# One of four masking chunks of a graph-attention stage moved from VectorE to GpSimd

## The chip, the cores and the metric

One core of a Trainium2 chip runs the whole program. The metric is the device time of one execution in microseconds (us). The engines are called as in the profile: PE (TensorE; PEld is its weight load), DVE (VectorE), ACT (ScalarE), POOL (GpSimd), SP (SyncE, here only an issuer of transfers; SPq is its queue).

## What is computed

A graph network of four layers on 3125 nodes and 100000 edges, of which only the first matters here. It is a stack of three graph-attention layers, and each does this:

```python
z = h @ W.T + b
e = leaky_relu(concat([z[src], z[dst]]) @ aW.T + ab, 0.01)[:, 0]
m = segment_max(e, dst)
ex = exp(e - m[dst])
alpha = ex / segment_sum(ex, dst)
return segment_sum(alpha[:, None] * z[src], dst)
```

## The kernel before

**Dense attention.** The kernel does not walk over edges here. It keeps a matrix of edge counts, sources by targets, in HBM, and computes a weight for every pair of a source and a target. A score depends on the source by one number and on the target by two, so that the exponent is a maximum of two sums: with s_low and s_rest of the source and two rows (shift_1, shift_2) of the targets, weight = exp(max(shift_1 + s_rest, shift_2) + s_low). It is clipped to at most 1 (a pair without an edge could otherwise be large) and multiplied by the count of edges, which is 0 for most pairs.

**Tiles and chunks.** `attention_layer` (line 899) is called once for each of the three layers. After a search for the maxima (line 1013, on DVE alone, 25 groups) comes the dense part: 25 source tiles of 128 rows (NT = 25), each cut into four chunks of target columns, `CUTS = (0, 512, 1536, 2560, 3125)`, so 512, 1024, 1024 and 565 columns. For tile s and chunk c there are four steps, each an instruction on its engine, and a fifth for the transfers:

- top (line 1030, DVE): `tops` = max(shift_1 + s_rest, shift_2), a scalar_tensor_tensor with two inputs in SBUF;
- exponentials (line 1074, ACT): exp in place in `tops`;
- mask (line 1039, DVE): `probs` = min(`tops`, 1) * `counts`, again a scalar_tensor_tensor with two inputs in SBUF;
- add_up (line 1106, PE): matmuls of z with `probs`, summed over the tiles in PSUM, two matmul records for each block of 512 columns;
- load_counts (line 949, SP): the counts of tile s + 1 into the same columns, once mask(s, c) is done.

`tops`, `probs` and `counts` are single buffers: top(s + 1, c) waits for mask(s, c), mask(s + 1, c) waits for add_up(s, c) (semaphore `used`) and for the load of the counts (semaphores `counts_in`), add_up(s, c) waits for mask(s, c). The semaphore `masked` counts all masks in order; DVE, PE and SP wait on it.

**Order on DVE.** A tile interleaves four tops with four masks two chunks back (`back`, line 941): top(s,0), mask(s-1,2), top(s,1), mask(s-1,3), top(s,2), mask(s,0), top(s,3), mask(s,1).

**POOL.** In the same stages POOL moves records of an edge table that a later part of the program needs. `StagedRows.scatter` (lines 477 to 485) waits for a load of 268 KB that SP issued (line 474) and issues four indirect DMAs of 128 rows (line 483). A layer's block on POOL is 6 of these jobs that go with the search and 14 that go with the dense tiles (`MOVED_DENSE`: in the layers 0 and 1 the even tiles and tile 11), with no other wait between them (lines 1091 and 1092); SP issues the loads for them before the counts of the tiles in `MOVED_DENSE` (line 974).

Of the kernel before, what the change touches and what calls it, by code (L numbers as in the profile page):

```python
# [10 lines left out]
ALU = mybir.AluOpType  # L11
# [10 lines left out]
NT = N // TN  # L22
# [28 lines left out]
MOVED_SEARCH = 6  # L51
MOVED_DENSE = ((11, *range(0, NT, 2)), (11, *range(0, NT, 2)), (0, 1, 2, 4, 6, 8, 9, 10, 12, 14, 16, 18, 20, 22))
# [8 lines left out]
NQ = len(CUTS) - 1  # L61
# [45 lines left out]
@contextmanager  # L107
def semaphores(nc, tag):

    held = []  # L110

    def sem(name):
        held.append(nc.alloc_semaphore(f"{tag}_{name}"))
        return held[-1]

    yield sem
    nc.clear_and_free_semaphores(held)
    nc.all_engine_barrier()  # L118
# [780 lines left out]
def attention_layer(k, layer, att):  # L899
# [10 lines left out]
    nc = k.nc  # L910
    tag, last_layer = f"a{layer}", layer == 2
    PER_BANK = 7
    with ExitStack() as ctx, semaphores(nc, tag) as sem:
        sb = lambda name, shape, dt=FP32: ctx.enter_context(nc.sbuf_tensor(f"{tag}_{name}", shape, dt))

# [3 lines left out]
        marks, marks_in, staged = att.marks_now, att.marks_in, att.staged  # L919
# [3 lines left out]
        counts, probs = sb("counts", [P, N]), sb("probs", [P, N])  # L923
        tops = sb("tops", [P, NPAD])
        chunk = [slice(a, b) for a, b in zip(CUTS, CUTS[1:])]
# [2 lines left out]
        shifts_in = [sem(f"shifts_in{c}") for c in range(NQ)]  # L928
        counts_in = [sem(f"counts_in{c}") for c in range(NQ)]
        topped, raised, masked, used = (sem(n) for n in ("topped", "raised", "masked", "used"))  # L930
        sums_taken, turned = sem("sums_taken"), sem("turned")
        sums = k.psum_cols(0, D + 1, N)
        sums_t = s_all[0:D + 1, 0:N]
# [3 lines left out]
        w_score, floor = sb("w_score", [D + 1, D]), sb("floor", [D + 1, 1])  # L937
        z_ready, sums_taken_act = sem("z_ready"), sem("sums_taken_act")
        TAKE = 3 * BANK

        def back(s, c):

            return (s, c - 2) if c >= 2 else (s - 1, c + NQ - 2)

        with nc.Block() as block:
            @block.sync
            def _(sp):
                def load_counts(s, c):
                    sp.dma_start(counts[:, chunk[c]], att.counts[s * P:(s + 1) * P, chunk[c]]).then_inc(counts_in[c], 16)

                sp.dma_start(s_all, att.score_rows[0, :].partition_broadcast(P)).then_inc(s_in, 16)
                with nc.allow_non_contiguous_dma(reason="a few thousand scores"):
                    sp.dma_start(d_group[:, :], att.score_rows[1, :].rearrange("(g p) -> p g", p=P)[0:GROUP, :])\
                        .then_inc(d_in, 16)
                for c in range(NQ):
                    load_counts(0, c)
                late = range(EARLY_MARKS, NGROUP // MARK_LOADS) if layer == 0 else ()
                for y in late:
                    att.load_marks(sp, y)
                    staged.load(sp)  # L960
                for _ in range(MOVED_SEARCH - len(late)):
                    staged.load(sp)

                sp.wait_ge(shift_step, 3)
                sp.dma_start(att.shift_rows.rearrange("a (g p) -> (a g) p", p=GROUP), shifts_t[:, 0:GROUP])\
                    .then_inc(rows_out, 16)
                sp.wait_ge(rows_out, 16)
                for c in range(NQ):
                    a, b = CUTS[c], CUTS[c + 1]
                    for to, row in ((shift_1, 0), (shift_2, 1)):  # L970
                        sp.dma_start(to[:, a:b], att.shift_rows[row, a:b].partition_broadcast(P))\
                            .then_inc(shifts_in[c], 16)
                for s in range(NT):
                    if s in MOVED_DENSE[layer]:
                        staged.load(sp)
                    for c in range(NQ):
                        if s + 1 < NT:

                            sp.wait_ge(masked, (s + 1) * NQ + c + 1)
                            load_counts(s + 1, c)  # L980

            @block.vector
            def _(dve):
                v, chain = nc.vector, Chain(dve, step)
                for sm in (raised, masked, used):
                    dve.sem_inc(sm, NQ)
                v.memset(shifts[:, :], 0.0)
                if not last_layer:
                    chain.link(v.memset(w_next[:, :], 0.0))
# [36 lines left out]

                def top(s, c):
                    cols = chunk[c]
                    dve.wait_ge(masked, s * NQ + c + 1)
                    v.scalar_tensor_tensor(tops[:, cols], shift_1[:, cols], s_rest[:, s:s + 1], shift_2[:, cols],  # L1030
                                           ALU.add, ALU.max).then_inc(topped, 1)

                def mask(s, c):
                    cols = chunk[c]
                    dve.wait_ge(raised, s * NQ + c + 1 + NQ)
                    dve.wait_ge(counts_in[c], s * 16 + 16)

                    dve.wait_ge(used, s * NQ + c + 1)
                    v.scalar_tensor_tensor(probs[:, cols], tops[:, cols], 1.0, counts[:, cols], ALU.min, ALU.mult)\  # L1039
                        .then_inc(masked, 1)  # L1040

                def tile(s, first=False):
                    for c in range(NQ):
                        if first:

                            dve.wait_ge(shifts_in[c], 32)
                        top(s, c)
                        if c >= 2 or not first:
                            mask(*back(s, c))

                for s in range(NT):
                    tile(s, s == 0)
                mask(NT - 1, NQ - 2)
                mask(NT - 1, NQ - 1)

                dve.wait_ge(used, NT * NQ + NQ)
                if last_layer:
                    v.tensor_copy(sums_t[:, 0:TAKE], sums[:, 0:TAKE]).then_inc(sums_taken, 1)
                else:
                    v.tensor_scalar(sums_t[:, 0:TAKE], sums[:, 0:TAKE], floor[:, :], 0.0, ALU.add, ALU.max)\  # L1060
                        .then_inc(sums_taken, 1)
                for b in range(0, NT, PER_BANK):
                    dve.wait_ge(turned, b // PER_BANK + 1)
                    n = min(PER_BANK, NT - b)
                    v.tensor_copy(k.acc[0:TN, b:b + n, 0:RESULT],
                                  k.psum[0:TN, b // PER_BANK, 0:n * RESULT].rearrange("p (t c) -> p t c", c=RESULT))

# [20 lines left out]

            @block.gpsimd
            def _(pool):  # L1090
                for _ in range(MOVED_SEARCH + len(MOVED_DENSE[layer])):
                    staged.scatter(pool)
                if last_layer:
                    staged.finish(pool)

            @block.tensor
            def _(pe):
                pe.wait_ge(shift_step, 1)
                nc.tensor.transpose(k.psum[0:2 * NGROUP, 7, 0:P], shifts[:, :], k.ident[:, :]).then_inc(shift_step, 1)  # L1099

                def add_up(s, c):

                    pe.wait_ge(masked, s * NQ + c + 1 + NQ)
                    for a in range(CUTS[c], CUTS[c + 1], BANK):
                        b = min(a + BANK, N)
                        last = nc.tensor.matmul(sums[:, a:b], k.z[:, s, 0:D + 1], probs[:, a:b], start=s == 0, stop=True,  # L1106
                                                skip_group_check=True)
                    last.then_inc(used, 1)

                if layer:  # L1110
                    pe.wait_ge(z_ready, 1)
                for s in range(NT):
                    for c in range(NQ):
                        add_up(s, c)

                pe.wait_ge(sums_taken, 1)
                if not last_layer:
                    pe.wait_ge(w_ready, 1)
                for t in range(NT):
                    at = (t % PER_BANK) * RESULT  # L1120
                    to, tile = k.psum[0:TN, t // PER_BANK, at:at + RESULT], sums_t[:, t * TN:(t + 1) * TN]
                    if t == TAKE // TN:
                        pe.wait_ge(sums_taken_act, 1)
                    if last_layer:
                        last = nc.tensor.transpose(to, tile, k.ident[0:D + 1, 0:D + 1])
                    else:
                        last = nc.tensor.matmul(to, tile, w_next[:, :], start=True, stop=True)
                    if t % PER_BANK == PER_BANK - 1 or t == NT - 1:
                        last.then_inc(turned, 1)
# [1064 lines left out]
```

## Time and profile before

| | us |
|---|---|
| device time, median of 3 runs (lowest, highest) | 4458.94 (4453.23, 4469.04) |
| the profiled execution: its span | 4502.7 |
| busy in the span: PE / DVE / ACT / POOL | 3132.8 / 3224.2 / 1435.4 / 1405.7 |
| a_probs (line 1039), 300 instructions, busy | 290.6 |
| a_tops on DVE (line 1030), 300 instructions, busy | 309.3 |
| records scattered on POOL (line 483), 192 + 96 instructions, busy | 327.6 + 166.6 |

The span is the one profiled execution from its first to its last instruction; it is the only time of that execution at hand, and lies 43.8 us (1.0%) above the median of the timed runs. A difference worked out from the profile is therefore added to the median as it is. Busy time of an engine that others wait for counts; idle time of another engine costs nothing. In the rows further down, "x" is a count, the number behind the bar is busy time and mean ns of one instruction, and "idle before" is how long the engine had been idle ahead of the instruction and for what it waited.

### The profile page before, as it was taken

What the parts mean: (1) busy time and instruction counts of PE and PEld (TensorE: products, weight loads), DVE (VectorE), ACT (ScalarE), POOL (GpSimd) and SP (SyncE); (2) the same over time, 40 slices, a digit from 0 to 9 for tenths busy, and PEclk for the clock granted to TensorE, in tenths of its full rate; (3) what the DMA queues carried; (4) which work ended last, traced back from release to release, by engine and by line L of the source; (5) the groups of instructions that cost most, each with busy time, mean ns of one, the idle gap of its engine ahead of it and who ended that gap; (6) DMA issues with size and microseconds to landing.
All of it is one profiled execution on the core that took longest, in us unless ns stands there. A gap on an engine that the chain in (4) does not pass through costs nothing. (4 is left out here: it accounts for less than half of the span.)

```text
span 4502.7 us, 84639 instructions
## 1 busy us (share of the span) xinstructions
PE 3132.8 (70%) x29061; PEld 2437.5 (54%) x29061; DVE 3224.2 (72%) x7791; ACT 1435.4 (32%) x2737; POOL 1405.7 (31%) x1198
## 2 busy tenths in 40 slices
PE   0087777777238348158499985588888769959995
PEld 0054444444102112112499984287888769959995
DVE  7766666665489699699577763377767579967886
ACT  0034444444025125035399981233333200000000
POOL 0055555555264454554000000266666300000000
PEclk9978888888569679579699996599999879979997
DMA  8845555545458358267377740111111024413331
GB/s 323 322 129 143 153 144 148 157 131 149 147 172 264 114 166 263 88 200 246 106 221 221 222 148 12 56 24 23 24 23 24 14 67 111 109 28 102 88 91 47
DMA packets 413507, 587.19 MB, mean 130 GB/s; under 512 B 76420, under 2 KB 301787, under 8 KB 412709
## 3 DMA queue, kind: packets, MB, share of 16 engines
q1 hardware_dynamic: 366005, 447.98, 34.2%
q0 software_dynamic: 37728, 66.91, 5.5%
q10 hardware_dynamic: 9360, 66.90, 3.7%
q8 instruction: 246, 4.03, 0.4%
q14 instruction: 168, 1.38, 0.1%
HBM read 340.05 MB, written 234.93 MB: 128 GB/s over the span
## 5 line engine op out<-in xcount | busy, mean ns | idle before, releaser
L846 POOL DMA_INDIRECT slots<-bc_rec,idx x496 | 484.6, 977 | 410.4 <-ACT bc_rec L807 294.4
L1284 POOL DMA_INDIRECT rp_rows<-rel_rows,slot_rel x390 | 412.1, 1057 | 431.7 <-POOLq L118 182.3
L1106 PE MATMUL psum<-a_probs,z 128*65 128x512 f32 (+1 forms) x1050 | 445.7, 557 | 145.0 <-DVE a_probs L1039 145.0
L1320 DVE TENSOR_SCALAR rp_hot_src<-rp_key_rows,lane 128x384 bf16<-128x384 f16 x1560 | 383.5, 317 | 202.0 <-issue 88.5
L1534 PE MATMUL psum<-rel_pieces,rp_hot_src 128*128 128x192 bf16 x4680 | 452.1, 249 | 94.3 <-issue 75.8
L1074 ACT ACTIVATE a_tops<-a_tops,a_s_low 128x1024 f32<-128x1024 f32 (+2 forms) x300 | 284.1, 947 | 569.6 <-DVE a_tops L1030 569.1
L1534 PEld LDWEIGHTS psum<-rel_pieces,rp_hot_src 128*128 128x128 bf16 x4680 | 390.4, 99 | 128.8 <-issue 107.0
L483 POOL DMA_INDIRECT slots<-h,idx x192 | 327.6, 1706 | 352.3 <-DMA h<-recs 304.1
L1106 PEld LDWEIGHTS psum<-a_probs,z 128*65 128x65 f32 x1050 | 121.8, 137 | 469.4 <-DVE a_probs L1039 301.5
L703 DVE TENSOR_SCALAR bc_first_t<-bc_ramp,bc_key_t 128x128 f16<-128x128 f16 x500 | 136.5, 273 | 307.8 <-PE psum L729 172.7
L1030 DVE SCALAR_TENSOR_TENSOR a_tops<-table,a_s_rest,big 128x1024 f32<-128x1024 f32 (+2 forms) x300 | 309.3, 1031 | 32.8 <-DMA big<-shift_rows 32.8
L729 PE MATMUL psum<-bc_first_s,bc_first_t 128*128 128x512 f16 x1000 | 220.2, 382 | 104.5 <-DVE bc_first_s L704 62.8
L1039 DVE SCALAR_TENSOR_TENSOR a_probs<-a_tops,a_counts 128x1024 f32<-128x1024 f32 (+2 forms) x300 | 290.6, 970 | 0.0
L1568 PE MATMUL psum<-ep_msg,ep_hot_dst 128*84 128x131 f32 x1950 | 278.4, 278 | 7.7 <-ACT ep_msg L1463 5.7
L1568 PE MATMUL psum<-sp_msg,sp_hot_dst 128*84 128x128 f32 x1950 | 280.6, 281 | 0.0
L1568 PE MATMUL psum<-sq_msg,sq_hot_dst 128*84 128x128 f32 x1950 | 272.0, 276 | 0.0
L704 DVE TENSOR_SCALAR bc_first_s<-bc_ramp,bc_key_s,bc_base_s 128x625 f16<-128x625 f16 x500 | 241.0, 482 | 0.8 <-issue 0.6
L1541 PE MATMUL psum<-far_pieces,sq_hot_src 128*128 128x128 bf16 x2925 | 217.7, 220 | 28.8 <-DMA sq_hot_src<-hot_rows 28.8
L1099 PE MATMUL psum<-ident,a_shifts 128*50 128x128 f32 x3 | 1.2, 411 | 331.3 <-DVE a_shifts L1021 331.3
L1541 PE MATMUL psum<-edge_pieces,ep_hot_src 128*128 128x131 bf16 x2925 | 229.1, 223 | 1.3 <-ACT ep_hot_src L1480 1.2
L792 ACT ACTIVATE bc_counts<-psum 128x625 f32<-128x625 f32 x125 | 88.2, 706 | 439.0 <-PE psum L739 232.2
L1568 PEld LDWEIGHTS psum<-ep_msg,ep_hot_dst 128*84 128x84 f32 x1950 | 221.7, 154 | 10.2 <-DVE ep_hot_dst L1329 9.9
(438 smaller groups left out, 6855.1 us busy)
## 6 DMA issues: line engine op xcount, KB each, us to landing
a_counts<-edge_counts SPq DMA_DIRECT2D x150, 512.0 KB
slots<-big ACTq DMA_DIRECT2D x65, 1005.0 KB
ep_rec<-slots SPq DMA_DIRECT2D x65, 1005.0 KB, 6.2
edge_counts<-bc_counts SPq DMA_DIRECT2D x12, 3125.0 KB
hot_rows<-ep_hot_src SPq DMA_DIRECT2D x325, 96.0 KB, 4.5
sp_hot_src<-hot_rows SPq DMA_DIRECT2D x325, 96.0 KB, 2.0
sq_hot_src<-hot_rows SPq DMA_DIRECT2D x325, 96.0 KB, 2.0
a_counts<-edge_counts SPq DMA_DIRECT2D x75, 282.5 KB
```

What stands on the lines that cost most here:

```text
L483: pool.indirect_dma_start(k.slots, bass.IndirectOffsetOnAxis(k.idx[:, at:at + 1], 0), self.rows[y][:, t, :], None).then_inc(self.scattered ...
L704: last = v.tensor_scalar(to_s[:, u, :], ramp[:, :], column(key_s, t), column(base_s, j), ALU.subtract, ALU.is_equal)
L846: pool.indirect_dma_start(k.slots, bass.IndirectOffsetOnAxis(k.idx[:, first + t:first + t + 1], 0), rec[:, j, t, :], None).then_inc(scatte ...
L1030: v.scalar_tensor_tensor(tops[:, cols], shift_1[:, cols], s_rest[:, s:s + 1], shift_2[:, cols], ALU.add, ALU.max).then_inc(topped, 1)
L1039: v.scalar_tensor_tensor(probs[:, cols], tops[:, cols], 1.0, counts[:, cols], ALU.min, ALU.mult)\
L1074: nc.scalar.activation(tops[:, cols], tops[:, cols], ACT.Exp, bias=s_low[:, s:s + 1])\
L1106: last = nc.tensor.matmul(sums[:, a:b], k.z[:, s, 0:D + 1], probs[:, a:b], start=s == 0, stop=True, skip_group_check=True)
L1284: pool.indirect_dma_start(rows[:, n % ROW_SLOTS, s, 0:width], None, table, bass.IndirectOffsetOnAxis(k.slot_rel[:, at:at + 1], 0))\
L1320: last = v.tensor_scalar(hot_src[:, n % HOT_SLOTS, rel, :], key_rows[:, n % 2, :], k.lane[:, rel:rel + 1], None, ALU.is_equal)
L1534: last = nc.tensor.matmul(to, hot_src[:, n % HOT_SLOTS, r, s * P:(s + 1) * P], pieces[:, row, r, :], start=s != 1 and r == 0, stop=True, s ...
L1541: last = nc.tensor.matmul(got[:, s, :], hot_src[:, n % HOT_SLOTS, s * P:(s + 1) * P], pieces[:, row, piece, :], start=s == 0 and piece == ...
L1568: last = nc.tensor.matmul(to[:, 0:D] if relations else to, hot_dst[:, y, s, :], got, start=first, stop=True, skip_group_check=True)
```

## The change

The third chunk (c = 2, columns 1536 to 2559) of every tile is masked on POOL, in two instructions (a tensor_scalar that clips in place in `tops`, and a tensor_tensor that multiplies by the counts into `probs`), with a semaphore between them. DVE keeps the masks of the chunks 0, 1 and 3. The waits are split: `masked` now counts DVE's three masks of a tile, `masked_pool` POOL's one; `wait_masked` picks between them for SP, DVE and PE. POOL's scatters of the dense part stand each behind the mask of its tile.

```diff
+    POOL_CHUNK = 2
+    MASKED_BY_DVE = [c for c in range(NQ) if c != POOL_CHUNK]
...
+        def wait_masked(eng, s, c):
+            if c == POOL_CHUNK:
+                eng.wait_ge(masked_pool, s + 2)
+            else:
+                eng.wait_ge(masked, (s + 1) * (NQ - 1) + MASKED_BY_DVE.index(c) + 1)
...
@@ SP, load_counts
-                            sp.wait_ge(masked, (s + 1) * NQ + c + 1)
+                            wait_masked(sp, s, c)
...
@@ DVE
-                for sm in (raised, masked, used):
+                for sm in (raised, used):
                     dve.sem_inc(sm, NQ)
+                dve.sem_inc(masked, NQ - 1)
+                dve.sem_inc(masked_pool, 1)
...
                 def top(s, c):
-                    dve.wait_ge(masked, s * NQ + c + 1)
+                    wait_masked(dve, s - 1, c)
...
-                        if c >= 2 or not first:
+                        if (c >= 2 or not first) and back(s, c)[1] != POOL_CHUNK:
                             mask(*back(s, c))
...
-                mask(NT - 1, NQ - 2)
                 mask(NT - 1, NQ - 1)
...
@@ POOL
-                for _ in range(MOVED_SEARCH + len(MOVED_DENSE[layer])):
+                def mask(s):
+                    cols = chunk[POOL_CHUNK]
+                    pool.wait_ge(raised, s * NQ + POOL_CHUNK + 1 + NQ)
+                    pool.wait_ge(counts_in[POOL_CHUNK], s * 16 + 16)
+                    pool.wait_ge(used, s * NQ + POOL_CHUNK + 1)
+                    nc.gpsimd.tensor_scalar(tops[:, cols], tops[:, cols], 1.0, None, ALU.min).then_inc(clipped, 1)
+                    pool.wait_ge(clipped, s + 1)
+                    nc.gpsimd.tensor_tensor(probs[:, cols], tops[:, cols], counts[:, cols], ALU.mult)\
+                        .then_inc(masked_pool, 1)
+
+                for _ in range(MOVED_SEARCH):
                     staged.scatter(pool)
+                for s in range(NT):
+                    mask(s)
+                    if s in MOVED_DENSE[layer]:
+                        staged.scatter(pool)
...
@@ PE, add_up
-                    pe.wait_ge(masked, s * NQ + c + 1 + NQ)
+                    wait_masked(pe, s, c)
```

## Rows read from the trace of the kernel before

**Rows 1.** Busy time by stretch: a search with the nodes before it, then a dense stage.

```profile
core 0: us, PE busy (x) PEld busy (x) DVE busy (x) ACT busy (x) POOL busy (x), PEclk, DMA share, GB/s
1160.00:1299.00 139.00, 7.72 (x31) 5.91 (x31) 99.37 (x85) 1.98 (x2) 68.10 (x34) 0.50 0.38 123
1299.00:1487.00 188.00, 145.81 (x343) 39.74 (x344) 182.15 (x200) 94.71 (x100) 79.14 (x55) 0.97 0.84 258
```

**Rows 2.** What DVE waited for, 1299 to 2135 us: total us, times, longest.

```profile
DVE a_tops L1030 <- DMA big<-shift_rows: 32.8, 9, 6.4
```

**Rows 3.** Instructions in order of time, 1324 to 1333 us (start, us, engine line).

```profile
1324.31 0.75 DVE L1030 SCALAR_TENSOR_TENSOR a_tops<-table,a_s_rest,big 128x512 f32<-128x512 f32 x1
...
1324.98 1.22 DVE L1039 SCALAR_TENSOR_TENSOR a_probs<-a_tops,a_counts 128x1024 f32<-128x1024 f32 x1
...
1325.51 1.52 POOL L483 DMA_INDIRECT slots<-h,idx  x1 [10.03 <-DMA h<-recs]
1326.11 1.28 DVE L1030 SCALAR_TENSOR_TENSOR a_tops<-table,a_s_rest,big 128x1024 f32<-128x1024 f32 x1
...
1327.31 0.75 DVE L1039 SCALAR_TENSOR_TENSOR a_probs<-a_tops,a_counts 128x565 f32<-128x565 f32 x1
1327.34 1.55 POOL L483 DMA_INDIRECT slots<-h,idx  x1 [0.30 <-issue]
...
1327.96 1.29 DVE L1030 SCALAR_TENSOR_TENSOR a_tops<-table,a_s_rest,big 128x1024 f32<-128x1024 f32 x1
...
1329.16 0.69 DVE L1039 SCALAR_TENSOR_TENSOR a_probs<-a_tops,a_counts 128x512 f32<-128x512 f32 x1
1329.19 1.49 POOL L483 DMA_INDIRECT slots<-h,idx  x1 [0.30 <-issue]
...
1329.76 0.81 DVE L1030 SCALAR_TENSOR_TENSOR a_tops<-table,a_s_rest,big 128x565 f32<-128x565 f32 x1
...
1330.48 1.23 DVE L1039 SCALAR_TENSOR_TENSOR a_probs<-a_tops,a_counts 128x1024 f32<-128x1024 f32 x1
...
1331.61 0.76 DVE L1030 SCALAR_TENSOR_TENSOR a_tops<-table,a_s_rest,big 128x512 f32<-128x512 f32 x1
```

**Rows 4.** Groups by shape, 1280 to 2180 us, all three dense stages.

```profile
L483 POOL DMA_INDIRECT slots<-h,idx x168 | 285.3, 1698 | 264.4 <-DMA h<-recs 222.1 <-issue 42.4
L1030 DVE SCALAR_TENSOR_TENSOR a_tops<-table,a_s_rest,big 128x1024 f32<-128x1024 f32 x150 | 192.5, 1283 | 14.5 <-DMA big<-shift_rows 14.5
L1039 DVE SCALAR_TENSOR_TENSOR a_probs<-a_tops,a_counts 128x1024 f32<-128x1024 f32 x150 | 183.2, 1223 | 0.0
L1074 ACT ACTIVATE a_tops<-a_tops,a_s_low 128x1024 f32<-128x1024 f32 x150 | 172.4, 1149 | 183.1 <-DVE a_tops L1030 183.1
...
L1013 DVE CUSTOM_DVE_ANT_0 a_tops<-marks_now,table 125x3200 f32<-125x3200 uint8 x28 | 97.6, 3485 | 6.9 <-issue 6.9
```

**Rows 5.** POOL in order of time: one scatter within the search, one behind it.

```profile
1284.68 3.11 POOL L483 DMA_INDIRECT slots<-h,idx  x1 [0.30 <-issue]
...
1292.77 0.96 POOL L483 DMA_INDIRECT slots<-h,idx  x1 [0.30 <-issue]
```

**Rows 6.** POOL's own computing instructions, whole program, by shape.

```profile
L266 POOL IOTA all_rows<- 128x3200 int16 x1 | 2.9, 2887 | 0.0
...
L269 POOL TENSOR_SCALAR_AFFINE_SELECT ident<-ident 128x128 f32<-128x128 f32 x1 | 0.3, 284 | 0.0
...
L261 POOL MEMSET ident<- 128x128 f32 x1 | 0.2, 204 | 0.3 <-POOLq L2187 0.3
...
L2187 POOL MEMSET const-float32-0.0<- 128x1 f32 x1 | 0.1, 98 | 0.3 <-issue 0.3
```

**Rows 7.** SP in order of time: loads of records in two tiles with jobs.

```profile
1321.15 0.43 SPq L474 DMA_DIRECT2D h<-recs  x1
1335.75 0.43 SPq L474 DMA_DIRECT2D node_midT<-recs  x1
```

**Rows 8.** PE's weight loads in order of time, from the third dense stage's start.

```profile
1958.61 0.23 PEld L1106 LDWEIGHTS psum<-a_probs,z 128*65 128x65 f32 x1 [0.62 <-issue]
1959.46 0.14 PEld L1106 LDWEIGHTS psum<-a_probs,z 128*65 128x65 f32 x1 [0.62 <-issue]
1959.89 0.14 PEld L1106 LDWEIGHTS psum<-a_probs,z 128*65 128x65 f32 x1 [0.29 <-issue]
```

More of the change, by code:

```diff
@@ L930, in attention_layer @@
         topped, raised, masked, used = (sem(n) for n in ("topped", "raised", "masked", "used"))
+        masked_pool, clipped = sem("masked_pool"), sem("clipped")
         sums_taken, turned = sem("sums_taken"), sem("turned")
```

## The prediction, made before the changed kernel was run

> **What bounds the kernel now.** I began with the busy time by stretch, since the change touches one kind of stage only. In the dense stage DVE is busy 182.15 of 188 us, PE 145.81, ACT 94.71 and POOL 79.14 [rows 1]; there are three such stages of nearly the same length, one eighth of the span. Next the list of what DVE waited for: in these stretches its longest entry is the load of the shift rows at each start, 32.8 us in 9 waits [rows 2], and no entry is a wait for ACT, PE or a count inside the tiles. So DVE sets the pace. Then the instructions in order of time: from top(s,0) at 1324.31 to the next one at 1331.61 the eight DVE instructions take 7.30 us [rows 3], less than the sum of their durations, since the record of one begins about 0.08 before that of the last one ends. The loads of records two tiles apart, at 1321.15 and 1335.75, give the same: 14.60 for two [rows 7]. What a mask of 1024 columns occupies is thus not its 1.22 us but the step from its start to the next start: 1324.98 to 1326.11, 1.13 us [rows 3].
>
> **What goes.** One such mask in each of 75 tiles: DVE's tile falls from 7.30 to 6.17 us, 85 us in all, if nothing else holds it.
>
> **What comes: POOL's two instructions.** The trace has no clip and no product on POOL, so I bound them by what POOL does compute [rows 6]. A memset of one column takes 98 ns, of 128 columns 204; an iota of 3200 columns 2887, so (2887 - 98) / 3200 = 0.87 ns a column; an affine_select, which reads and writes each element, (284 - 98) / 128 = 1.45 ns a column. The clip of 1024 columns lies between 0.10 + 0.89 = 0.99 us and 0.10 + 1.49 = 1.59; it is a read and a write without affine_select's test, so nearer the lower end, and I take 1.1. The product reads two elements for each it writes: at the least 0.99, with two passes at iota's rate 0.10 + 2 x 0.89 = 1.88, with two at affine_select's 0.10 + 2 x 1.49 = 3.07; I take 2.3, a little under the middle of the last two, as there is no test. Together 3.4 us a tile (2.9 to 4.7), for 1.13 us taken from DVE. The Trainium skill, GPSIMD Engine Reference, section "Elementwise — side-by-side cycle accounting", gives 4497 ns for a float32 tensor_tensor of 2048 columns, which would make about 2.25 us here, an estimate; by it the sum would come out 0.05 us a tile lower.
>
> **What POOL and DVE do to each other.** This I read from the scatters. A scatter takes 0.96 us when DVE is idle, and 3.11 plus 0.30 of issue when DVE runs the search's instructions of 3.49 us [rows 5, 4]: one scatter for each DVE instruction. In the dense stage the three in [rows 3] end at 1327.03, 1328.89 and 1330.68, each 0.92 or 0.93 us after a top began, 1326.11, 1327.96 and 1329.76, whatever the scatter's own start was. So a scatter that begins under a DVE instruction with two SBUF inputs waits until that has ended and then needs its usual time. It reads only an index a partition, and DVE's steps are not longer for it, so the trace doesn't show the other direction: whether a long POOL read holds DVE. The bounds are 0 and POOL's whole 3.4 us a tile. The Trainium skill, SBUF — State Buffer, section "SBUF: two separate sides", says it does: one shared pair of ports, held for a whole instruction by a VectorE instruction with two SBUF inputs or by a GpSimd instruction that reads SBUF, whichever came first. No row here shows that half of it.
>
> **The sum, first way (they exclude each other).** All seven DVE instructions left in a tile have two SBUF inputs. Tile = 6.17 + 1.1 + 2.3 + 0.2 for two changes of hands (DVE loses its overlap of about 0.1 each time) = 9.8 us, against 7.30.
>
> **The sum, second way (only POOL waits).** `tops` is one buffer, so chunk 2 is a ring: top(s,2) 1.28, exp 1.15 [rows 4], clip 1.1, product 2.3, and top(s+1,2) again. Before, DVE's order hid it. With some 0.1 for each of four semaphores it is 6.2 us, and POOL waits twice for the DVE instruction under way, about 0.5 each (half of 0.65 to 1.2): 7.2 us. That is for a tile without a job. With one, four scatters stand between this product and the next clip, in POOL's one queue: at the pace of [rows 3], (1.55 + 0.30) or (1.49 + 0.30) each, they take 7.3 us, longer than the 2.6 us until tops is ready again, and the ring is 7.3 + 0.5 + 1.1 + 0.1 + 0.5 + 2.3 = 11.8 us. Queued behind the late clip are the product, and behind that DVE's top(s+1,2) with all its later tops, PE's add_up of chunks 2 and 3, and SP's load of the next counts. A stage: 14 x 11.8 + 11 x 7.2 = 244 us, 9.8 a tile. Both ways meet at the same figure, so it does not hang on the unseen half of the exclusion.
>
> **What lies beside it.** SP now waits for POOL before counts(s+1,2) and, behind it in the same queue, counts(s+1,3) and the next load of records. A load of records took from 1321.15 to 1325.51, 4.4 us [rows 7, 3]; the counts of a chunk are twice as large. The clip waits for them as well, so they may replace the 2.6 us of top and exp in the ring of a tile without a job by 4.5 or so. I add 0.1 us a tile of the possible 0.8 (11 tiles of 25, 1.9 us). PE needs 12 records of 0.43 us in a tile [rows 8], about 5.5 us, and hides in 9.8. ACT (3.8 us a tile) hides too. The six search jobs are issued before the first mask, as before, and the last job of a stage ends beside the turning of the sums, so the edges cost nothing beyond a microsecond or two. The split semaphores are as many waits as before; the new `clipped` wait is in the 0.1s above. Nothing outside these stages changes.
>
> Sum: (9.9 - 7.3) x 75 = +195 us. Against the profiled execution that is 4502.7 + 195 = 4698; against the median of the runs 4458.9 + 195 = 4654, and the forecast is in terms of the median. A measurement of this kernel can tell about 0.3%, 13 us, from no change.
>
> **The rivals.**
> (A) The forecast, chance 0.70. With POOL's pair at 2.9 us it gives 4459 + 195 - 0.5 x 75 = 4616; at 4.7 it gives 4654 + 1.3 x 75 = 4751.
> (B) POOL's computing instructions run freely beside DVE, and only the ring and the queue behind the scatters cost. For it: the scatters show only an index read being held. Against: a product reads far more than an index. The ring is 6.2 without a job and 7.3 + 1.1 + 0.1 + 2.3 = 10.8 with one: 14 x 10.8 + 11 x 6.2 = 219 us against 182.5, +37 a stage, +110: 4569. Chance 0.17.
> (C) PE's clock falls. Now it is granted 0.97 in the dense stage and 0.50 in the search before it [rows 1]. If the gaps that POOL's late product leaves bring it to the lower level (1.2 GHz), weight loads are 0.85 us apart (1958.61 to 1959.46) in place of 0.43 [rows 8]; 12 of them and the two short ones make 10.6 us, more than the tile: +3.3 x 75 = +248, 4707. Against: PE would still be busy for more than half of the time. Chance 0.07.
> (D) Faster: POOL is hidden and DVE's 6.17 is the pace, -1.13 x 75 = -85, 4374. It decides on POOL's work in a stage: 25 pairs and 14 jobs must fit in 25 x 6.17 = 154 us to have all of it, and in 182 to have any. With 3.4 us and jobs at the unhindered pace (4 x 1.26 = 5.0) that would be 85 + 71 = 156; at the pace of [rows 3] it is 85 + 102 = 187, already over. It needs free running of both kinds, and the ring of the tiles with jobs (5.0 + 3.4 = 8.5) made up by those without. The scatters in [rows 3] speak against it. Chance 0.06.
>
> **The numbers.** The forecast is A's, 4654. The range takes in B at the low end with a little room, C, and A's upper bound: 4555 to 4755; outside are D and some of A's and B's tails. Faster by over 0.3%: 0.05, nearly all of D. Within 0.3%: 0.03, D in part and the easiest end of B. Slower: 0.92.
>
> **What would show it.** Right: dense stages of about 245 us; DVE no longer busy throughout, or with single tops and masks whose records are stretched to 3 us or more where they met POOL's product (exclusion, both directions); starts of top(s,0) about 10 us apart, farther in tiles with a job; a new wait of DVE's top of chunk 2 for POOL; the other stages unchanged. A top or mask that runs its 1.3 us in the middle of POOL's product would refute the exclusion and leave B. The whole would be wrong if POOL's pair took 2 us or less, or if the scatters fell to 0.96 us beside DVE; and the cost would be higher if PE's granted clock in the dense stage fell below 0.9.

## The result, and the profile after

The changed kernel takes 4778.4 us (median of 4 runs, 4775.7 to 4782.2) against 4458.9 of the kernel before: ratio 1.073, 95% interval 1.071 to 1.074, +319.5 us. The sign was forecast, the size not: +195 was expected and 4755 was the upper end of the range.

Busy time by stretch of the changed kernel: its three dense stages, with a search and the nodes between the first two.

```profile
core 0: us, PE busy (x) PEld busy (x) DVE busy (x) ACT busy (x) POOL busy (x), PEclk, DMA share, GB/s
1281.00:1577.00 296.00, 180.56 (x350) 52.57 (x350) 167.36 (x176) 94.73 (x101) 227.43 (x109) 0.78 0.52 165
1577.00:1708.00 131.00, 9.77 (x56) 8.45 (x56) 96.42 (x86) 2.81 (x2) 83.53 (x38) 0.52 0.24 71
1708.00:2006.00 298.00, 177.71 (x350) 51.36 (x350) 166.05 (x176) 95.05 (x101) 227.09 (x106) 0.78 0.51 163
2140.00:2437.00 297.00, 179.12 (x350) 51.72 (x350) 166.62 (x176) 94.89 (x101) 227.17 (x106) 0.78 0.51 163
```

Against [rows 1] the stage went from 188 to 296 us and DVE from busy all the time to 167 of 296. POOL, at 227, is the busiest engine, and is still idle for a quarter. PE's granted clock fell from 0.97 to 0.78. The stretch between is no longer than before. From here on a stage is measured in one way for every kernel: from its first top to the DVE instruction that takes the sums out of PSUM, mean of the three. It is 190.5 us before and 296.7 after; 3 x 106.2 = 319 us, the whole difference.

Groups by shape, 1280 to 2500 us, and below them what waited for whom in the same stretch (total us, times, longest).

```profile
L483 POOL DMA_INDIRECT slots<-h,idx x161 | 295.1, 1833 | 79.8 <-issue 41.1 <-DMA h<-recs 35.4 <-PE psum L1131 2.4
L1107 POOL TENSOR_SCALAR a_tops<-a_tops 128x1024 f32<-128x1024 f32 x75 | 219.8, 2931 | 166.0 <-DMA a_counts<-edge_counts 94.8 <-PE psum L1131 35.3 <-ACT a_tops L1085 34.7
L1042 DVE SCALAR_TENSOR_TENSOR a_tops<-table,a_s_rest,big 128x1024 f32<-128x1024 f32 x150 | 211.5, 1410 | 364.7 <-POOL a_probs L1109 351.2 <-DMA big<-shift_rows 13.6
L1109 POOL TENSOR_TENSOR a_probs<-a_tops,a_counts 128x1024 f32<-128x1024 f32 x75 | 177.9, 2372 | 6.3
```

```profile
DVE a_tops L1042 <- POOL a_probs L1109: 351.2, 71, 7.4
PE psum L1131 <- POOL a_probs L1109: 325.9, 75, 7.9
POOL a_tops L1107 <- DMA a_counts<-edge_counts: 94.8, 23, 5.5
POOL a_tops L1107 <- PE psum L1131: 35.3, 9, 3.9
```

DVE's top of chunk 2 now waits for POOL's product in 71 of 75 tiles, 4.9 us each: the new wait that was named. The product takes 2.37 us, as costed (2.3). The clip takes 2.93 us where 1.1 was put, and that is no effect of waiting: where DVE was idle it takes 2.79.

How a tile goes shows in the order of time. First one without a job; from product to product it takes 9.48 us (1398.41 to 1407.89).

```profile
1398.41 2.34 POOL L1109 TENSOR_TENSOR a_probs<-a_tops,a_counts 128x1024 f32<-128x1024 f32 x1
...
1400.78 1.28 DVE L1042 SCALAR_TENSOR_TENSOR a_tops<-table,a_s_rest,big 128x1024 f32<-128x1024 f32 x1 [6.36 <-POOL a_probs L1109]
...
1402.10 1.15 ACT L1085 ACTIVATE a_tops<-a_tops,a_s_low 128x1024 f32<-128x1024 f32 x1 [7.52 <-DVE a_tops L1042]
...
1404.44 2.72 DVE L1042 SCALAR_TENSOR_TENSOR a_tops<-table,a_s_rest,big 128x512 f32<-128x512 f32 x2
1404.67 3.14 POOL L1107 TENSOR_SCALAR a_tops<-a_tops 128x1024 f32<-128x1024 f32 x1 [3.92 <-PE psum L1131]
...
1407.89 2.34 POOL L1109 TENSOR_TENSOR a_probs<-a_tops,a_counts 128x1024 f32<-128x1024 f32 x1
```

The ring of the forecast is there, but its first part is another one: exp is done at 1403.25, yet the clip starts at 1404.67, when PE's add_up of this chunk ends. So it is in 9 tiles; in 23 others the clip starts when the counts land. PE began those four matmuls at 1400.80 after an idle of 7.27 us, and its weight loads there stand 0.85 us apart, the spacing of the lower clock level (1.2 GHz) in [rows 8]:

```profile
1401.71 0.23 PEld L1131 LDWEIGHTS psum<-a_probs,z 128*65 128x65 f32 x1 [0.62 <-issue]
1402.57 0.23 PEld L1131 LDWEIGHTS psum<-a_probs,z 128*65 128x65 f32 x1 [0.62 <-issue]
1403.42 0.23 PEld L1131 LDWEIGHTS psum<-a_probs,z 128*65 128x65 f32 x1 [0.62 <-issue]
```

The next tile has a job. First the view of POOL alone, then that of DVE alone:

```profile
1407.89 2.34 POOL L1109 TENSOR_TENSOR a_probs<-a_tops,a_counts 128x1024 f32<-128x1024 f32 x1
1410.39 2.10 POOL L483 DMA_INDIRECT slots<-node_midT,idx  x1 [0.16 <-issue]
1412.80 2.04 POOL L483 DMA_INDIRECT slots<-node_midT,idx  x1 [0.30 <-issue]
1415.14 2.22 POOL L483 DMA_INDIRECT slots<-node_midT,idx  x1 [0.30 <-PE psum L1131]
1417.66 0.98 POOL L483 DMA_INDIRECT slots<-node_midT,idx  x1 [0.30 <-issue]
1418.67 2.79 POOL L1107 TENSOR_SCALAR a_tops<-a_tops 128x1024 f32<-128x1024 f32 x1
1421.55 2.34 POOL L1109 TENSOR_TENSOR a_probs<-a_tops,a_counts 128x1024 f32<-128x1024 f32 x1
```

```profile
1415.78 0.74 DVE L1051 SCALAR_TENSOR_TENSOR a_probs<-a_tops,a_counts 128x565 f32<-128x565 f32 x1
1423.92 1.28 DVE L1042 SCALAR_TENSOR_TENSOR a_tops<-table,a_s_rest,big 128x1024 f32<-128x1024 f32 x1 [7.39 <-POOL a_probs L1109]
```

From product to product this tile takes 13.66 us, with four scatters in 8.3 between product and clip. DVE has nothing to do from 1416.5 to 1423.9 and the clip still needs 2.79.

### The profile page after: what moved, and what is told of

It is laid out like the page before. It is cut to its first block and busy times, and to the rows that moved or that the text cites. A ratio compares the mean times of both kernels' runs of the same rounds, so it can differ in the third digit from the quotient of the medians.

```text
span 4774.0 us, 84717 instructions
## 1 busy us (share of the span) xinstructions
PE 3207.6 (67%) x29061; PEld 2460.1 (52%) x29061; DVE 3173.5 (66%) x7716; ACT 1440.5 (30%) x2737; POOL 1822.7 (38%) x1348
## 5 line engine op out<-in xcount | busy, mean ns | idle before, releaser
L1131 PE MATMUL psum<-a_probs,z 128*65 128x512 f32 (+1 forms) x1050 | 537.4, 672 | 372.8 <-POOL a_probs L1109 325.9
L1042 DVE SCALAR_TENSOR_TENSOR a_tops<-table,a_s_rest,big 128x1024 f32<-128x1024 f32 (+2 forms) x300 | 324.0, 1099 | 383.9 <-POOL a_probs L1109 351.2
L1309 POOL DMA_INDIRECT rp_rows<-rel_rows,slot_rel x390 | 398.4, 1022 | 417.4 <-POOLq L118 181.2
L1131 PEld LDWEIGHTS psum<-a_probs,z 128*65 128x65 f32 x1050 | 155.6, 169 | 755.1 <-POOL a_probs L1109 393.6
L1559 PE MATMUL psum<-rel_pieces,rp_hot_src 128*128 128x192 bf16 x4680 | 437.8, 248 | 74.7 <-issue 46.9
L483 POOL DMA_INDIRECT slots<-h,idx x192 | 347.0, 1807 | 172.3 <-DMA h<-recs 120.0
L1107 POOL TENSOR_SCALAR a_tops<-a_tops 128x1024 f32<-128x1024 f32 x75 | 219.8, 2931 | 166.0 <-DMA a_counts<-edge_counts 94.8
L704 DVE TENSOR_SCALAR bc_more_s<-bc_ramp,bc_key_s,bc_base_s 128x625 f16<-128x625 f16 x500 | 224.0, 448 | 0.4 <-issue 0.4
```

The source lines that it names most:

```text
L483: pool.indirect_dma_start(k.slots, bass.IndirectOffsetOnAxis(k.idx[:, at:at + 1], 0), self.rows[y][:, t, :], None).then_inc(self.scattered ...
L704: last = v.tensor_scalar(to_s[:, u, :], ramp[:, :], column(key_s, t), column(base_s, j), ALU.subtract, ALU.is_equal)
L1309: pool.indirect_dma_start(rows[:, n % ROW_SLOTS, s, 0:width], None, table, bass.IndirectOffsetOnAxis(k.slot_rel[:, at:at + 1], 0))\
L1559: last = nc.tensor.matmul(to, hot_src[:, n % HOT_SLOTS, r, s * P:(s + 1) * P], pieces[:, row, r, :], start=s != 1 and r == 0, stop=True, s ...
```

## The experiments

Two theories explained about equally well a tile of 11.4 us (the mean distance from one first top to the next). *Ring*: POOL's chain of chunk 2 (its product, then what frees the clip, clip, product), with the scatters in its queue, sets the pace. *Exclusion*: POOL and DVE take turns, so all their work adds up, 6.17 + 2.79 + 2.34 + 0.2 = 11.5. The stage lengths in one place (us; before 190.5, after 296.7):

```
without the clip            219.7      control: jobs first, before 190.4
clip twice                  369.7      jobs first, changed kernel  250.0
waits behind the clip       281.7      control + free clips        217.4
chunk 0 on POOL             240.9      control + free products     268.3
clip as multiplication      280.8      control + free memsets      190.5
```

The kernel before took 4484 us where it ran beside the first three kernels, 4458 beside the next four and 4162 beside the last three. A dense stage in which DVE is undisturbed did not take part in that: it is 190.4 us long in the second group (jobs first, kernel before) and 190.5 in the third (free memsets). So times are compared only with the kernel before of the same group.

**The clip left out and doubled.**

```diff
-                    nc.gpsimd.tensor_scalar(tops[:, cols], tops[:, cols], 1.0, None, ALU.min).then_inc(clipped, 1)
-                    pool.wait_ge(clipped, s + 1)
```

> The changed kernel without POOL's clip: the product alone (the weights are then not cut at 1, a part of the computation that is left out). Ring theory: POOL's chain of chunk 2 sets the pace, so a tile without a job falls from 9.5 us to about 3.9 + 2.34 = 6.3, one with a job from 13.2 to about 10.4, a stage from 297 us to about 218, the time from 4778 to about 4545. Exclusion theory (POOL and DVE take turns, all their work adds up): a tile is 6.17 + 2.34 + 0.1 = 8.6 with or without a job, a stage about 220: the same total, but another pattern of the tiles.

Measured 4572.9 us, +89 over the kernel before (ratio 1.020, 1.017 to 1.023), so 230 less than the change costs. The total came out (stage 219.7 for 218), the pattern did not follow the ring alone: most tiles take 8.3 or 8.6 us, with or without a job. DVE's view shows why.

```profile
1438.88 4.04 DVE L1042 SCALAR_TENSOR_TENSOR a_tops<-table,a_s_rest,big 128x512 f32<-128x512 f32 x2
...
1449.01 2.89 DVE L1051 SCALAR_TENSOR_TENSOR a_probs<-a_tops,a_counts 128x565 f32<-128x565 f32 x1
```

```profile
1438.91 2.92 POOL L1107 TENSOR_TENSOR a_probs<-a_tops,a_counts 128x1024 f32<-128x1024 f32 x1 [3.73 <-DMA a_counts<-edge_counts]
...
1448.74 2.55 POOL L1107 TENSOR_TENSOR a_probs<-a_tops,a_counts 128x1024 f32<-128x1024 f32 x1
```

With the ring shorter, DVE works while POOL multiplies, and pays. The two tops at 1438.88 take 4.04 us where they take 1.94 without a product beside them; the mask of 565 columns takes 2.89 where 0.74 is usual. The product is longer by no more than the rest of the DVE instruction under way. So in this kernel the tile is the one that exclusion gives (8.6), and not the ring's 6.3 and 10.4: with the clip gone, exclusion by the product is what keeps the kernel slower than before.

```diff
-                    pool.wait_ge(clipped, s + 1)
+                    pool.wait_ge(clipped, 2 * s + 1)
+                    nc.gpsimd.tensor_scalar(tops[:, cols], tops[:, cols], 1.0, None, ALU.min).then_inc(clipped, 1)
+                    pool.wait_ge(clipped, 2 * s + 2)
```

> The changed kernel with the clip done twice. Ring theory: + (2.79 to 3.14 + 0.09) us in each of 75 tiles, +215 to +240 us, about 5005; DVE's additional instructions do not grow in number and it idles longer. Should the clip's cost be hidden in part, less.

Measured 4988.7, +505 over the kernel before (1.113, 1.110 to 1.116), 185 more than the change costs; by the stages it is 3 x 73.0 = 219, and the profiled execution had the longest span of its runs (5026). The second clips take 2.78 us each, 2.9 a tile with the wait: nothing of them is hidden.

**The waits moved behind the clip.**

```diff
-                    pool.wait_ge(counts_in[POOL_CHUNK], s * 16 + 16)
-                    pool.wait_ge(used, s * NQ + POOL_CHUNK + 1)
                     nc.gpsimd.tensor_scalar(tops[:, cols], tops[:, cols], 1.0, None, ALU.min).then_inc(clipped, 1)
                     pool.wait_ge(clipped, s + 1)
+                    pool.wait_ge(counts_in[POOL_CHUNK], s * 16 + 16)
+                    pool.wait_ge(used, s * NQ + POOL_CHUNK + 1)
```

> The changed kernel with POOL's waits for the counts and for PE's add_up put between clip and product. Ring theory: in the 33 tiles without a job the clip starts 2.5 us after the product before it (top and exp) instead of 3.9, so 9.5 becomes about 8.0; tiles with a job do not change, as the scatters end later than either. 33 x 1.4 = -46 us, about 4732. Exclusion theory: no change, since all the work still adds up.

Measured 4763.1, +279 over the kernel before (1.062, 1.059 to 1.065): 40 less than the change costs, 45 by the stages. The sum came out by luck, for its parts did not. Tiles without a job fell only from 9.5 to 9.3, those with one from about 13.2 to 12.4.

```profile
1410.77 2.34 POOL L1109 TENSOR_TENSOR a_probs<-a_tops,a_counts 128x1024 f32<-128x1024 f32 x1
1415.70 3.81 POOL L1105 TENSOR_SCALAR a_tops<-a_tops 128x1024 f32<-128x1024 f32 x1 [2.59 <-ACT a_tops L1085]
1419.59 2.79 POOL L1109 TENSOR_TENSOR a_probs<-a_tops,a_counts 128x1024 f32<-128x1024 f32 x1
```

The clip starts 2.6 us after the product, as expected; but now it meets more of DVE's instructions and takes 3.81, and the product 2.79. Why scatters in tiles with a job got shorter here was not tried; they begin at another point of DVE's sequence.

**The jobs moved in front.** In the kernel before and in the changed one, the 14 jobs of a stage go ahead of its first mask (`MOVED_SEARCH = 20`, `MOVED_DENSE = ((), (), ())`).

> Control: the kernel before with the 14 jobs of a dense stage moved in front of its first mask (POOL's queue and SP's loads). What counts is the length of the dense stage in the trace, not the time, which grows by the moved jobs. Both theories: 190 us as before, DVE's 7.30 a tile.

> The changed kernel with the same move of the jobs: no scatter stands between two masks of POOL. Ring theory: every tile takes the 9.5 us that tiles without a job take now, a stage about 245 us instead of 297. Exclusion theory: the scatters cost DVE nothing, a tile is 6.17 + 2.79 + 2.34 + 0.2 = 11.5, a stage about 290.

The control's stages are 190.4 us with 7.3 a tile, as with the jobs in them (190.5): the scatters never cost DVE anything. The changed kernel's are 250.0, nearly all tiles 9.5 us. Exclusion had 290. This is the run that tells the two apart: the pace was the ring's, and the 14 jobs are worth 47 us a stage in it. (The times, 4651 and 4823, hold the moved jobs too.)

**POOL's instructions by themselves.** The control with 60 instructions a stage on tensors that nobody else uses. Shown is the kernel with clips. In the other two the line with `tensor_scalar` is `nc.gpsimd.tensor_tensor(idle_out, idle_a, idle_b, ALU.mult)` or `nc.gpsimd.memset(idle_out, 0.0)`, with the same semaphore behind it.

```diff
+        idle_a, idle_b = (k.x[:, t:t + 10, :].rearrange("p t c -> p (t c)") for t in (0, 10))
+        idle_out, idle_step = k.node_in[:, :, :].rearrange("p t c -> p (t c)"), sem("idle_step")
...
+                pool.wait_ge(raised, 1 + NQ)
+                for i in range(60):
+                    if i:
+                        pool.wait_ge(idle_step, i)
+                    nc.gpsimd.tensor_scalar(idle_out, idle_a, 1.0, None, ALU.min).then_inc(idle_step, 1)
```

> The control with 60 clips of 640 columns a stage on POOL, on tensors that nobody else uses, one behind the other, waiting for nothing but the clip before. Each should take about 0.1 + 640 x 2.63 ns = 1.8 us. Exclusion: the stage grows from 190 by 60 x 1.8 = 108 us to about 298. No contention: 190. What the changed kernel's trace shows (a DVE instruction of 1.28 us takes 1.9 under a clip): in between, some 20 to 30 us.

> The same with 60 products of 640 columns with two inputs, about 1.5 us each. Exclusion: the stage grows by 60 x 1.5 = 90 us to about 280. No contention: 190.

> As the free clips and products, with 60 memsets of 640 columns a stage, which only write. If DVE loses time only where both read through something shared, its tile stays 7.30 us; if the clip's 0.45 us of stretch came from its writes, DVE's instructions stretch here too.

Stages of 217.4, 268.3 and 190.5 us. DVE beside clips, then DVE beside products:

```profile
1421.74 1.73 DVE L1032 SCALAR_TENSOR_TENSOR a_tops<-table,a_s_rest,big 128x1024 f32<-128x1024 f32 x1
1423.39 0.68 DVE L1041 SCALAR_TENSOR_TENSOR a_probs<-a_tops,a_counts 128x512 f32<-128x512 f32 x1
1424.00 1.25 DVE L1032 SCALAR_TENSOR_TENSOR a_tops<-table,a_s_rest,big 128x565 f32<-128x565 f32 x1
```

```profile
1427.75 2.55 DVE L1032 SCALAR_TENSOR_TENSOR a_tops<-table,a_s_rest,big 128x1024 f32<-128x1024 f32 x1
1430.23 2.02 DVE L1041 SCALAR_TENSOR_TENSOR a_probs<-a_tops,a_counts 128x512 f32<-128x512 f32 x1
1432.17 2.07 DVE L1032 SCALAR_TENSOR_TENSOR a_tops<-table,a_s_rest,big 128x565 f32<-128x565 f32 x1
```

A clip of 640 columns (2.20 us on average) stretches one DVE instruction by 0.45 us and lets the next run as usual; (217.4 - 190.4) / 60 = 0.45. A product of 640 columns (2.13 us on average with its own wait, 1.55 the shortest) stretches every DVE instruction by about 1.3 while products run: a tile then takes 17.8 us, and (268.3 - 190.4) / 60 = 1.30. A memset costs DVE nothing: the 60 run for 41 us of a stage, and the tiles there stay at 7.3.

**The form of the clip.** The minimum replaced by a multiplication by 1, the cut left out: `ALU.mult` for `ALU.min` in the clip.

> The changed kernel with POOL's clip (minimum with 1) replaced by a multiplication by 1 in the same form of instruction; the cut at 1 is left out. If POOL's tensor_scalar is slow as a form, it takes 2.79 us again and the stage 297. If it is the minimum, it comes to about 1.1 us, the term of the prediction, and the stage falls by about 25 x 1.7 = 42 us.

They take 2.96 us each. It is the instruction's form, tensor_scalar with float32 on POOL, not the minimum. Nor is it that the clip works in place: the free clips write to another tensor, and the shortest of 640 columns takes 1.83 us where the shortest product takes 1.55. The stage was 280.8 and not 297; since the clip was no shorter, that gain is not the clip's. It lies in the scatters: within the stages they took 1.39 us on average against 1.67, and 56 x 0.28 = 16 us. Why they did is open; the kernel ran once, and the changed kernel not beside it.

**A smaller chunk.** `POOL_CHUNK = 0`, and DVE masks chunk 2 of the last tile at the end.

> The changed kernel with the first chunk (512 columns) on POOL in place of the third (1024). DVE then loses a step of 0.60 us a tile and does 6.70. Ring theory with the prices measured so far, halved: clip 1.45, product 1.2, four scatters 8.2. A tile with a job: 8.2 + 1.45 + 0.1 + 1.2 = 11.0. A tile without: the ring is 6 us, shorter than DVE's 6.70, which pays for contention 0.4 under the clip and up to 1.2 under the product, so 6.7 to 8.3. Stage 14 x 11.0 + 11 x (6.7 to 8.3) = 228 to 245 us against 190 before: +110 to +165 us in all over the kernel before, still slower than it. If it is rather the mere size of the chunk that was chosen wrong, it should come out at or under the kernel before.

Measured 4315.1 against 4161.9 of the kernel before in its group: +153 (1.037, 1.034 to 1.039). Stages 240.9; tiles with a job mostly 10.5, those without 8.1. Half the columns, half the loss, and no gain.

## Why the prediction was right and wrong

- **DVE bounds the stage, and a mask of 1024 columns is worth 1.13 us a tile.** The first half is right: with four masks and an idle POOL the tile is 7.30 (the control). The 85 us were never seen, since a wait took their place, and no kernel here has DVE undisturbed with three masks, so the 1.13 us is not shown by itself.
- **The product, 2.3 us.** Right: 2.34 alone, 2.37 on average.
- **The clip, 1.1 us (0.99 to 1.59).** This is the step that failed. It takes 2.79 alone and 2.93 on average, 1.8 times the upper bound. The bounds were taken from an iota, which reads nothing, and from an affine_select of 128 columns, and neither is this form. The doubled clip shows that such an instruction in the ring costs its full length. 1.83 us more in 75 tiles is +137 us, where measurement and forecast differ by +125.
- **The second way to the sum, the ring.** Right in kind: jobs first gives 9.5 us in nearly every tile and leaves DVE idle. With the measured clip in its own arithmetic it gives 14 x 13.5 + 11 x 8.9 = 287 us, plus the 8 by which a stage before was longer than 25 tiles (190.5 - 182.5): 295 against 296.7.
- **The first way, full exclusion.** As the pace of the changed kernel it is refuted by jobs first (250, not 290). That both ways gave 9.8 was a coincidence of the sizes put in. Of the exclusion itself the half that no row showed is true for the product and, in the changed kernel, hardly used: DVE is idle by then. For the clip it is true only in part. Of the 525 DVE instructions in the changed kernel's three stages 33 are over 0.4 us longer than usual, the longest 2.89 us, so the sign that was named, records of 3 us or more, did not appear.
- **What the prediction cites for the exclusion.** The Trainium skill, SBUF — State Buffer, "SBUF: two separate sides", says that a GpSimd instruction that reads SBUF keeps the shared pair for all of its length against a VectorE instruction with two SBUF inputs. The products nearly agree: about 1.3 us of stretch for each one of 640 columns, of which the shortest takes 1.55. The clips do not: 0.45 us of a clip that takes 2.20. That an instruction that only writes is free of it agrees with the memsets.
- **Counts and add_up in place of top and exp.** Seen, but costed at 0.1 us a tile, 7.5 in all; it is 50. That is the time by which the clip started after its exp had ended: 37 us in the 23 tiles in which the counts came last, 13 in the 9 in which add_up did. The wait from product to clip is 3.9 us in the tile without a job shown, not 2.6 plus half of a DVE instruction. PE's granted clock in the stage fell from 0.97 to 0.78, below the 0.9 named as a sign of more cost; at this place it can own no more than the 13 us, and no run changes it alone. As a pace of its own (rival C) it did not come: PE is busy for 181 of 296 us.
- **Four scatters in 7.3 us.** 8.3 in the tile shown. The forecast of such a tile came out nearly right with the measured clip only because 1 us too much stood beside it, the two waits of POOL for a DVE instruction: 7.3 + 0.5 + 0.5 against 8.3, with DVE idle. That is luck.
- **Rival B, POOL's computing instructions run freely beside DVE.** The free products refute it as a mechanism. Its sum with the measured clip would be 14 x 12.5 + 11 x 7.9 = 262 us a stage, 270 with the 8 us, against 296.7.
- **Rival D, faster.** Its condition, POOL's work within 25 x 6.17 = 154 us, fails by far: 227 us busy.
- **The range.** Its upper end used a pair of 4.7 us; the pair is 5.3.

No kernel tried beats the one before. The kernel without a clip shows why a shorter ring would not be enough: what DVE is spared is 1.13 us for a mask of 1024 columns, and a product of 1024 columns takes 2.1 us from it when the two meet (4.04 in place of 1.94, 2.89 in place of 0.74). The free products give the same, 1.30 us for 640 columns.

## What to carry to other kernels

Before work is moved from an engine that is always busy to one that is often idle, look at what else is in the idle engine's queue, and at the chain of single buffers through the moved step: here both were longer than the tile that was to be shortened. Price each new instruction by its own form on its own engine; an estimate from other forms of that engine was off here by a factor of 2.5, in the direction that hurts, and its upper bound by 1.8. And two theories that give the same sum are told apart by a kernel in which only one of them loses a term (here: the jobs moved away), not by more arithmetic.

## What the runs showed of the hardware that was not expected

On POOL the float32 tensor_scalar with one input (2.79 us for 1024 columns) is slower than the tensor_tensor with two (2.34 us). What they take from a DVE instruction with two inputs in SBUF goes the other way: 0.45 us for a clip of 640 columns, 1.30 us for a product, 0 for a memset of the same size (0.63 us).
